# A recurrent cell with two half-states: the order of the DMA queue at a block's edge, and how r and m of the second half are turned and summed

## Chip, cores and metric

One core of one Trainium2 chip runs the whole kernel. The metric is the device time of one execution in microseconds (us); smaller is better.

## The reference

The reference is a gated recurrence over 512 steps, for a batch of 8 and a state of 512, in float32. What is added at the end is the input itself:

```python
def step(h, x_t):
    fused = jax.nn.sigmoid(jnp.concatenate([x_t, h], axis=-1) @ w_W + w_b)
    hidden_state, output_state = jnp.split(fused, 2, axis=-1)
    memory_state = x_t @ wx_W + wx_b + hidden_state * (h @ wh_W + wh_b)
    h_new = output_state * h + (1.0 - output_state) * jnp.tanh(memory_state)
    return (h_new, h_new)
_, hs = jax.lax.scan(step, h0, xT)
return x + jnp.swapaxes(hs, 0, 1)          # x: (8, 512, 512)
```

Below, r is the gate `hidden_state`, z is `output_state`, and m is the memory state before its tanh.

## The kernel before

**Tiling.** The state lies across the 128 partitions in four chunks (KC = 4), two chunks to a half (o = 0 and 1). A step needs products of h with the weights of r, m and z. TensorE (PE) makes them with h as the stationary operand, so that batch rows come out in PSUM in four tiles of 32 rows; VectorE then transposes ("turns") 32x32 blocks so that the state lies across partitions again. r, m and z of the first half, and z of the second, are made with float32 products (line 265). r and m of the second half are made together from h cut into three bfloat16 parts (`products_of_parts`, line 274): their PSUM tile has, for each of 8 batch rows, three rows of partial sums (PARTS = 3), and for m a fourth row with the part of the input x. GpSimd cuts the parts of h (lines 539 and 541) and adds x to h for the output (line 549).

**A step on VectorE.** `turn_r`, `turn_m`, `turn_z(0)`, the scan that forms m of the first half (line 443), then `turn_rm` (line 432, 128 columns of the second half's r and m), `sum_r` (line 439, adds the three parts of r), `mix_h(0)` (line 457, the scan that makes h's first half), `turn_z(1)`, `mix_m_second` (line 449), and `mix_h(1)`. Between them ScalarE computes the sigmoids (lines 359, 363, 366) and tanh (line 372). `turn_rm` writes each turned row so that the four rows of one state element (three parts and x) lie side by side, which puts consecutive output elements four words (16 bytes) apart. `mix_m_second` then runs one scan over 64 columns, four for each of 16 elements: it adds up m's three parts with factors of one, multiplies the sum by sigmoid(r), and adds x's part.

**The order of a step on PE.** It waits for the first half of h, makes its products and those of its parts; waits for the second half of h; makes that half's products (r, m, z0), its parts' products, and z1; last come the products of x for a later group (line 256, `x_products`), which need no h. Then the next step begins.

**Groups and blocks.** Four steps are a group (RING), sixteen a block (STEPS); there are 32 blocks. x's products with the biases added (`xs_biased`, line 462, once a group) are sent by SP's DMA queue to device memory and back (`put_ahead`): one DMA out (`x_rows`, line 188), a wait for its landing, then twelve DMAs back (lines 193 and 197) that bring the rows to `ahead`, from which ScalarE puts them into PSUM (lines 348, 352, 356) before the products of a step are added. SP issues all of this in program order. In a block it issues: the load of x for the block after next into `x_sb` (line 221), the rows of the second group (`put_ahead`, slot 1), then for each group g the loads of `x_grp` (line 206) and the rows of a later group; at the end of the block it waits for GpSimd's sums and stores `y` (line 241). Then the next block's pass begins, with its `x_sb` load and its rows.

Of the kernel before, what the change touches and what calls it, by code (L numbers as in the profile page):

```python
# [6 lines left out]
ALU = mybir.AluOpType  # L7
ACT = mybir.ActivationFunctionType
AX = mybir.AxisListType

P = 128
Q = 32


def build(nc, x, h0, w_h, w_x, b_x, b_h, x_rows, out):
# [49 lines left out]
    with ctx:  # L65
        def sb(name, shape, dt=F32):
            return ctx.enter_context(nc.sbuf_tensor(name, shape, dt))

        def sem(name):
            return ctx.enter_context(nc.semaphore(name))  # L70
# [19 lines left out]
        turned_rm = sb("turned_rm", [P, 2, HB, ROWS])  # L90
        turned_z = sb("turned_z", [P, HALVES, HC, Q])
        pre_r = sb("pre_r", [P, HB])


        m_by = sb("m_by", [P, HB, PAIR])
        m_pre = sb("m_pre", [P, HB, PAIR])
        m_by_parts = sb("m_by_parts", [P, HB, ROWS])
        m_pre_parts = sb("m_pre_parts", [P, HB, ROWS])
# [61 lines left out]
        rm_turned = sem("rm_turned")  # L160
        z_turned = halves("z_turned")
        r_summed = sem("r_summed")
        x_product = sem("x_product")
        x_used = [sem(f"x_used{k}") for k in range(KC - 1)]
        x_biased = sem("x_biased")
# [33 lines left out]
        @block.sync  # L199
        def _(sp):  # L200
            sp.sem_inc(y_stored, 2 * 16)
            x_flat = x.rearrange("p c t b -> p c (t b)")
            out_flat = out.rearrange("p c t b -> p c (t b)")

            def load_x_grp(k, cols):
                sp.dma_start(x_grp[:, k], x_flat[:, k, cols]).then_inc(x_grp_loaded[k], 16)

            sp.dma_start(x_sb[:, :, 0:TOK], x_flat[:, :, 0:TOK]).then_inc(x0_loaded, 16)
            for k in range(KC):
                sp.dma_start(wx[:, k], w_x[:, k]).then_inc(wx_loaded[k], 16)  # L210
# [7 lines left out]
            with sp.Fori(0, BLOCKS) as i:  # L218
                cols = bass.ds(sp.snap((i + 2) % BLOCKS * TOK), TOK)
                sp.wait_ge(x_loaded, sp.snap(i * 16 + 16))  # L220
                sp.dma_start(x_sb[:, :, cols], x_flat[:, :, cols]).then_inc(x_loaded, 16)  # L221


                sp.wait_ge(x_biased, sp.snap(i * PER_BLOCK + 2))
                put_ahead(sp, 1, sp.snap((i * PER_BLOCK + 2) * 16))
                for g in range(PER_BLOCK):

                    turn = sp.snap(i * PER_BLOCK + (g + 1))
                    grp_cols = bass.ds(sp.snap((i * PER_BLOCK + (g + 3)) % GROUPS * GT), GT)
                    for k in range(KC):  # L230
                        if k < KC - 1:
                            sp.wait_ge(x_used[k], turn)
                        else:
                            sp.wait_ge(x_product, sp.snap(i * PER_BLOCK + (g + 3)))
                        load_x_grp(k, grp_cols)
                    if g < PER_BLOCK - 1:
                        sp.wait_ge(x_biased, sp.snap(i * PER_BLOCK + (g + 3)))
                        put_ahead(sp, g % SLOTS, sp.snap((i * PER_BLOCK + (g + 3)) * 16))
                sp.wait_ge(y_added, sp.snap(i * STEPS + 2 * STEPS))
                sp.sem_inc(y_taken, 1)  # L240
                sp.dma_start(out_flat[:, :, bass.ds(sp.snap(i * TOK), TOK)],  # L241
                             y[:, bass.ds(sp.snap(i % 2), 1)].rearrange("p a c t b -> p (a c) (t b)"))\
                    .then_inc(y_stored, 16)
# [102 lines left out]
        def _(act):  # L346
# [9 lines left out]
                act.activation(ps[:, Z_BANK[1], 0:W], ahead[:, slot, t, at:at + W], ACT.Copy).then_inc(z_ahead, 1)  # L356

            def reset_first():
                act.activation(m_by[:, :, 1].rearrange("p (c b) -> p c b", b=B), turned_r[:, :, 0:B], ACT.Sigmoid)\  # L359
                    .then_inc(r_ready[0], 1)  # L360

            def reset_second():
                act.activation(m_by_parts[:, :, PARTS], pre_r[:, :], ACT.Sigmoid).then_inc(r_ready[1], 1)  # L363
# [4 lines left out]

            def new(o, s):
                n_twice = h[:, (s - 1) % RING, o, 1:1 + REGION].rearrange("p (b c w) -> p c b w", c=HC, w=TRI)[:, :, :, 0::2]  # L370
                pre = (m_pre[:, :, 1], m_pre_parts[:, :, PARTS])[o].rearrange("p (c b) -> p c b", b=B)
# [51 lines left out]
        def _(dve):  # L423
# [17 lines left out]
            def mix_m_first():  # L441

                return dve.tensor_tensor_scan(m_pre[:, :, :].rearrange("p i w -> p (i w)"),
                                              m_by[:, :, :].rearrange("p i w -> p (i w)"),
                                              turned_m[:, 0].rearrange("p i w -> p (i w)"), 0.0, ALU.mult, ALU.add)

            def mix_m_second():

                return dve.tensor_tensor_scan(m_pre_parts[:, :, :].rearrange("p i w -> p (i w)"),  # L449
                                              m_by_parts[:, :, :].rearrange("p i w -> p (i w)"),  # L450
                                              turned_rm[:, 1].rearrange("p i w -> p (i w)"), 0.0, ALU.mult, ALU.add)

            def mix_h(o, s, nxt):

# [9 lines left out]
            def step(i, t0, s):  # L464
# [12 lines left out]
                mix_m_first().then_inc(m_pre_ready[0], 1)  # L477
# [3 lines left out]
                sum_r().then_inc(r_summed, 1)  # L481
                mix_h(0, s, nxt)
                dve.wait_ge(z_done[1], nxt)
                turn_z(1).then_inc(z_turned[1], 1)
                dve.wait_ge(r_ready[1], nxt)
                mix_m_second().then_inc(m_pre_ready[1], 1)
                mix_h(1, s, nxt)
                if s % RING == RING - 1:

# [4 lines left out]
                    add_bias(X_BANK)  # L494

            dve.memset(h[:, :, :, :], 0.0).then_inc(start_h, 1)
            dve.memset(m_by[:, :, :], 0.0).then_inc(constants, 1)
            dve.memset(m_by_parts[:, :, :], 0.0).then_inc(constants, 1)
            dve.memset(h_by[:, :, :, :], 0.0).then_inc(constants, 1)
            dve.wait_ge(constants, 3)  # L500
            dve.memset(m_by_parts[:, :, 1:PARTS], 1.0).then_inc(constants, 1)
            dve.memset(h_by[:, :, :, 1], -1.0).then_inc(constants, 1)
            dve.wait_ge(constants, 5)
            dve.wait_ge(h0_loaded, 16)
            dve.wait_ge(start_h, 1)

# [28 lines left out]
        def _(pool):  # L535
# [14 lines left out]
                                   xs_of, hs, ALU.add).then_inc(y_added, 1)  # L550

            pool.sem_inc(y_added, STEPS)
            pool.memset(ahead[:, :, :, :], 0.0).then_inc(ahead_cleared, 1)
            pool.wait_ge(bias_h_loaded, 16)
            pool.wait_ge(ahead_cleared, 1)
# [73 lines left out]
```

## Time and profile before

| | us |
|---|---|
| median of 3 runs | 1673.91 (1670.84 to 1674.57) |
| the profiled execution | 1674.5 |
| its span | 1672.7 |
| PE busy | 1627.8 (97%) |
| VectorE (DVE) busy | 1203.1 (72%) |
| ScalarE (ACT) busy | 890.7 (53%) |
| GpSimd (POOL) busy | 568.7 (34%) |

The busy times are of the profiled execution, and their shares are of its span. PE's busy time includes the modelled ends of its pipelined matmuls, so 97% does not by itself say that PE is the bound; PEld is PE's loading of stationary operands. SPq is SP's DMA queue. The mean granted clock of TensorE over the span was 0.996 of full speed.

### The profile page before, as it was taken

What the parts mean: (1) busy time and instruction counts of PE and PEld (TensorE: products, weight loads), DVE (VectorE), ACT (ScalarE), POOL (GpSimd) and SP (SyncE); (2) the same over time, 40 slices, a digit from 0 to 9 for tenths busy, and PEclk for the clock granted to TensorE, in tenths of its full rate; (3) what the DMA queues carried; (4) which work ended last, traced back from release to release, by engine and by line L of the source; (5) the groups of instructions that cost most, each with busy time, mean ns of one, the idle gap of its engine ahead of it and who ended that gap; (6) DMA issues with size and microseconds to landing.
All of it is one profiled execution on the core that took longest, in us unless ns stands there. A gap on an engine that the chain in (4) does not pass through costs nothing.

```text
span 1672.7 us, 211594 instructions
## 1 busy us (share of the span) xinstructions
PE 1627.8 (97%) x94336; PEld 1343.3 (80%) x94336; DVE 1203.1 (72%) x5272; ACT 890.7 (53%) x4621; POOL 568.7 (34%) x2571
## 2 busy tenths in 40 slices
PE   5999999999999999999999999999999999999998
PEld 3788888888888888888888888888888888888887
DVE  3677777777777777777777777777777777777776
ACT  2455555555555555555555555555555555555554
POOL 1233333333333333333333333333333333333333
PEclk8999999999999999999999999999999999999999
DMA  6111111111111111111111111111111111111111
GB/s 199 32 48 46 51 46 38 51 48 48 46 43 45 46 51 48 46 36 51 49 47 51 46 38 46 52 49 46 35 54 48 46 51 46 38 51 49 48 46 39
DMA packets 194889, 83.27 MB, mean 50 GB/s; under 512 B 123200, under 2 KB 194368, under 8 KB 194880
## 3 DMA queue, kind: packets, MB, share of 16 engines
q1 hardware_dynamic: 193824, 82.47, 18.3%
q10 hardware_dynamic: 1056, 0.67, 0.2%
q8 instruction: 6, 0.10, 0.0%
q14 instruction: 3, 0.02, 0.0%
HBM read 49.30 MB, written 33.75 MB: 50 GB/s over the span
## 4 chain that ended last, share of the span: by engine, by line
PE 72%; DMA 9%; SPq 9%; DVE 4%; issue 3%; ACT 1%; POOL 1%; ACTq 0%; POOLq 0%; DVEq 0%
PE ps L265 43%; PE ps L274 15%; PE ps L256 14%; DMA x_rows<-xs_biased 5%; SPq L197 4%; DMA ahead<-x_rows 3%; SPq L193 2%; SPq L241 1%; SPq L221 1%; DVE h L457 1%; DVE turned_rm L432 1%; DMA wx<-in_w_x 1%; ACT ps L348 1%; DVE m_pre_parts L449 1%; POOL y L549 0%
## 5 line engine op out<-in xcount | busy, mean ns | idle before, releaser
L265 PE MATMUL ps<-wh,h 128*8 128x64 f32 x65536 | 1209.2, 220 | 35.3 <-ACT ps L348 29.2
L265 PEld LDWEIGHTS ps<-wh,h 128*8 128x8 f32 x65536 | 963.2, 93 | 312.6 <-DVE h L457 290.2
L539 POOL TENSOR_TENSOR h<-h 128x16 f32<-128x16 f32 x1026 | 224.7, 219 | 1018.0 <-DVE h L457 1014.1
L274 PE MATMUL ps<-w_parts,h 128*24 128x128 bf16 x24576 | 532.8, 219 | 0.0
L274 PEld LDWEIGHTS ps<-w_parts,h 128*24 128x24 bf16 x24576 | 431.8, 121 | 0.0
L256 PE MATMUL ps<-wx,x_grp 128*32 128x384 f32 x4096 | 425.0, 486 | 0.0
L359 ACT ACTIVATE m_by<-turned_r 128x16 f32<-128x16 f32 x512 | 112.1, 219 | 541.0 <-DVE turned_r L425 541.0
L457 DVE TENSOR_TENSOR_SCAN h<-h_by,h 128x48 f32<-128x48 f32 x1024 | 259.3, 253 | 161.0 <-ACT h L372 161.0
L425 DVE STREAM_TRANSPOSE turned_r<-ps 128x64 f32<-128x64 f32 x512 | 127.8, 250 | 242.6 <-PE ps L265 229.9
L366 ACT ACTIVATE h_by<-turned_z 128x16 f32<-128x16 f32 x1024 | 227.8, 222 | 99.0 <-DVE turned_z L436 63.5
L541 POOL TENSOR_TENSOR h<-h 128x16 f32<-128x16 f32 x1026 | 224.5, 219 | 80.3
L436 DVE STREAM_TRANSPOSE turned_z<-ps 128x64 f32<-128x64 f32 x1024 | 243.1, 237 | 3.0 <-PE ps L265 3.0
L432 DVE STREAM_TRANSPOSE turned_rm<-ps 128x128 f32<-128x128 f32 x512 | 218.2, 426 | 0.2 <-PE ps L274 0.2
L348 ACT ACTIVATE ps<-ahead 128x192 f32<-128x192 f32 x513 | 171.0, 333 | 22.7 <-DMA ahead<-x_rows 22.7
L449 DVE TENSOR_TENSOR_SCAN m_pre_parts<-m_by_parts,turned_rm 128x64 f32<-128x64 f32 x512 | 153.9, 301 | 19.9 <-ACT m_by_parts L363 18.9
L363 ACT ACTIVATE m_by_parts<-pre_r 128x16 f32<-128x16 f32 x512 | 120.8, 236 | 62.2 <-DVE pre_r L439 17.4
L352 ACT ACTIVATE ps<-ahead 128x128 f32<-128x128 f32 x513 | 143.5, 280 | 0.0
L372 ACT ACTIVATE h<-m_pre_parts 128x32 f32<-128x32 f32 x512 | 127.2, 248 | 28.7
L549 POOL TENSOR_TENSOR y<-x_sb,h 128x32 f32 x512 | 138.0, 270 | 0.7
L372 ACT ACTIVATE h<-m_pre 128x32 f32<-128x32 f32 x512 | 124.5, 243 | 0.0
L428 DVE STREAM_TRANSPOSE turned_m<-ps 128x64 f32<-128x64 f32 x512 | 119.7, 234 | 1.7 <-PE ps L265 1.7
L439 DVE TENSOR_REDUCE pre_r<-turned_rm 128x16 f32<-128x48 f32 x512 | 104.1, 203 | 17.6
(30 smaller groups left out, 422.1 us busy)
## 6 DMA issues: line engine op xcount, KB each, us to landing
x_rows<-xs_biased SPq DMA_DIRECT2D x128, 192.0 KB, 1.9
ahead<-x_rows SPq DMA_DIRECT2D x512, 32.0 KB
ahead<-x_rows SPq DMA_DIRECT2D x1024, 8.0 KB
x_sb<-in_x SPq DMA_DIRECT2D x34, 256.0 KB, 3.3
x_grp<-in_x SPq DMA_DIRECT2D x516, 16.0 KB, 1.7
out_h<-y SPq DMA_DIRECT2D x32, 256.0 KB, 2.7
wx<-in_w_x SPq DMA_DIRECT2D x4, 768.0 KB, 9.1
wh<-in_w_h SPq DMA_DIRECT2D x4, 512.0 KB, 7.3
```

Source lines behind the costliest of these rows:

```text
L256: mm = pe.matmul(ps[Q * j:Q * (j + 1), bank, 0:COLS], stands, wx[:, k, j, :], start=(k == 0), stop=(k == KC - 1), tile_position=(0, Q * j))
L265: mm = pe.matmul(ps[Q * j:Q * j + B, bank, 0:W], h_of(s - 1, k), wh[:, k, j, at:at + W], start=False, stop=(k == KC - 1), skip_group_check ...
L274: mm = pe.matmul(ps[Q * j:Q * j + PARTS * B, RM_BANK, 0:2 * W], parts_of(s - 1, k), w_parts[:, k, part, j], start=False, stop=(k == KC - 1 ...
L348: act.activation(ps[:, 0:GATES, 0:W], ahead[:, slot, t, 0:GATES * W].rearrange("p (g n) -> p g n", n=W), ACT.Copy).then_inc(first_ahead, 1)
L366: act.activation(h_by[:, o, :, 2].rearrange("p (b c) -> p c b", c=HC), turned_z[:, o, :, 0:B], ACT.Sigmoid)\
L372: act.activation(n_twice, pre.unsqueeze(3).to_broadcast([P, HC, B, 2]), ACT.Tanh)\
L432: return dve.transpose(turned_rm.rearrange("p g (c b) w -> p (g c) w b", b=B), ps[:, RM_BANK, 0:2 * W].rearrange("p (c q) -> p c q", q=Q))
L436: return dve.transpose(turned_z[:, o], ps[:, Z_BANK[o], 0:W].rearrange("p (c q) -> p c q", q=Q))
L449: return dve.tensor_tensor_scan(m_pre_parts[:, :, :].rearrange("p i w -> p (i w)"), m_by_parts[:, :, :].rearrange("p i w -> p (i w)"), tur ...
L457: dve.tensor_tensor_scan(h[:, s % RING, o, 0:REGION], h_by[:, o].rearrange("p i w -> p (i w)"), h[:, (s - 1) % RING, o, 1:1 + REGION], 0.0 ...
L539: pool.tensor_tensor(mid(1, s, o), mid(0, s, o), mid_top(0, s, o), ALU.subtract).then_inc(left_once[o], 1)
L541: pool.tensor_tensor(mid(2, s, o), mid(1, s, o), mid_top(1, s, o), ALU.subtract)\
```

## The change

Three things are changed.

1. **SP's order at a block's edge.** The pass over a block now begins with the wait for the biased sums and `put_ahead` of slot 1 (the rows); after it come the store of the previous block's `y`, and then the load into `x_sb`. The first block's pass is written out ahead of the loop, and the last block's store stands behind it.
2. **r and m of the second half.** `turn_rm` writes its 128 columns in the order in which they come, adjacent. One reduction (`sum_rm`) adds up the three parts of both r and m: it reads 96 elements, its three terms 8 words (32 bytes) apart, and writes 32. The scan that forms m of the second half has 32 columns instead of 64, like that of the first half.
3. **x's part of m.** Since the scan needs it beside the sum, GpSimd brings it there: in each step, once `turn_rm` is done, it adds zeros to 16 elements of `turned_rm` and writes them into `summed` (`x_moved`). The scan on VectorE waits for that as well as for the sum. On GpSimd this stands ahead of the cutting of h into parts.

```diff
+            def store_y(i, which):
+                sp.wait_ge(y_added, held(sp, i * STEPS + 2 * STEPS))
+                sp.sem_inc(y_taken, 1)
+                sp.dma_start(out_flat[:, :, bass.ds(held(sp, i * TOK), TOK)],
+                             y[:, bass.ds(which, 1)].rearrange("p a c t b -> p (a c) (t b)")).then_inc(y_stored, 16)
+            def pass_of(i, before):
+                sp.wait_ge(x_biased, held(sp, i * PER_BLOCK + 2))
+                put_ahead(sp, 1, held(sp, (i * PER_BLOCK + 2) * 16))
+                if before is not None:
+                    store_y(before, held(sp, before % 2))
+                cols = bass.ds(held(sp, (i + 2) % BLOCKS * TOK), TOK)
+                sp.wait_ge(x_loaded, held(sp, i * 16 + 16))
                 sp.dma_start(x_sb[:, :, cols], x_flat[:, :, cols]).then_inc(x_loaded, 16)
...
+            pass_of(0, None)
+            with sp.Fori(1, BLOCKS) as i:
+                pass_of(i, sp.snap(i - 1))
+            store_y(BLOCKS - 1, (BLOCKS - 1) % 2)
...
             def turn_rm():
-                return dve.transpose(turned_rm.rearrange("p g (c b) w -> p (g c) w b", b=B),
-                                     ps[:, RM_BANK, 0:2 * W].rearrange("p (c q) -> p c q", q=Q))
+                return dve.transpose(turned_rm[:, :, :], ps[:, RM_BANK, 0:2 * W].rearrange("p (c q) -> p c q", q=Q))
...
-            def sum_r():
-                return dve.tensor_reduce(pre_r[:, :], turned_rm[:, 0, :, 0:PARTS], AX.X, ALU.add)
+            def sum_rm():
+                return dve.tensor_reduce(summed[:, :, :, 0].rearrange("p g (c b) -> p (g c) b", b=B),
+                                         turned_rm.rearrange("p c (w b) -> p c b w", b=B)[:, :, :, 0:PARTS],
+                                         AX.X, ALU.add)
...
                 dve.wait_ge(r_ready[1], nxt)
-                mix_m_second().then_inc(m_pre_ready[1], 1)
+                dve.wait_ge(x_moved, nxt)
+                dve.wait_ge(r_summed, nxt)
+                mix_m(1, summed[:, 1]).then_inc(m_pre_ready[1], 1)
                 mix_h(1, s, nxt)
...
                 for s in range(STEPS):
+                    pool.wait_ge(rm_turned, held(pool, t0 + (s + 1)))
+                    pool.tensor_tensor(summed[:, 1, :, 1].rearrange("p (c b) -> p c b", b=B),
+                                       turned_rm[:, HC:2 * HC, PARTS * B:ROWS * B], nothing[:, :, :], ALU.add)\
+                        .then_inc(x_moved, 1)
```

## Rows read from the trace of the kernel before

**Rows 1.** Chain of waits, steady stretch: start us, length us, what.

```profile
920.91 0.34 PE ps L274 x24
...
949.20 0.33 PE ps L274 x24
```

**Rows 2.** Timeline of PE alone: start us, length us, engine line op out<-in.

```profile
903.08 0.51 PE L256 MATMUL ps<-wx,x_grp 128*32 128x384 f32 x4
...
903.40 0.51 PE L256 MATMUL ps<-wx,x_grp 128*32 128x384 f32 x4
903.74 0.25 PE L265 MATMUL ps<-wh,h 128*8 128x64 f32 x4
```

**Rows 3.** Timeline of one step, idle time before in brackets.

```profile
902.55 0.25 DVE L436 STREAM_TRANSPOSE turned_z<-ps 128x64 f32<-128x64 f32 x1
...
902.72 0.18 DVE L443 TENSOR_TENSOR_SCAN m_pre<-m_by,turned_m 128x32 f32<-128x32 f32 x1
...
902.86 0.42 DVE L432 STREAM_TRANSPOSE turned_rm<-ps 128x128 f32<-128x128 f32 x1
...
903.31 0.20 DVE L439 TENSOR_REDUCE pre_r<-turned_rm 128x16 f32<-128x48 f32 x1
903.43 0.25 DVE L457 TENSOR_TENSOR_SCAN h<-h_by,h 128x48 f32<-128x48 f32 x1
...
903.76 0.22 POOL L539 TENSOR_TENSOR h<-h 128x16 f32<-128x16 f32 x1 [1.39 <-DVE h L457]
903.84 0.29 DVE L449 TENSOR_TENSOR_SCAN m_pre_parts<-m_by_parts,turned_rm 128x64 f32<-128x64 f32 x1
...
904.44 0.26 DVE L457 TENSOR_TENSOR_SCAN h<-h_by,h 128x48 f32<-128x48 f32 x1 [0.32 <-ACT h L372]
904.64 0.56 DVE L462 TENSOR_TENSOR xs_biased<-ps,bias_x 128x384 f32<-128x384 f32 x1
...
904.76 0.86 PE L265 MATMUL ps<-wh,h 128*8 128x64 f32 x48
```

**Rows 4.** Chain of waits at the edge of a block.

```profile
905.84 0.66 SPq L241
...
914.82 1.59 DMA ahead<-x_rows
```

**Rows 5.** Who waited for whom: us in total, times, longest us.

```profile
PEld ps L265 <- DVE h L457: 290.2, 509, 1.5
...
PE ps L265 <- ACT ps L348: 29.2, 29, 14.4
ACT ps L348 <- DMA ahead<-x_rows: 22.7, 31, 1.0
```

**Rows 6.** Timeline of SP's queue in an ordinary group.

```profile
918.38 0.33 SPq L188 DMA_DIRECT2D x_rows<-xs_biased  x1
...
923.71 0.65 SPq L197 DMA_DIRECT2D ahead<-x_rows  x2
```

**Rows 7.** Groups by line and shape: xcount | busy us, mean ns | idle before.

```profile
L432 DVE STREAM_TRANSPOSE turned_rm<-ps 128x128 f32<-128x128 f32 x512 | 218.2, 426 | 0.2 <-PE ps L274 0.2
L449 DVE TENSOR_TENSOR_SCAN m_pre_parts<-m_by_parts,turned_rm 128x64 f32<-128x64 f32 x512 | 153.9, 301 | 19.9 <-ACT m_by_parts L363 18.9
...
L425 DVE STREAM_TRANSPOSE turned_r<-ps 128x64 f32<-128x64 f32 x512 | 127.8, 250 | 242.6 <-PE ps L265 229.9
L372 ACT ACTIVATE h<-m_pre_parts 128x32 f32<-128x32 f32 x512 | 127.2, 248 | 28.7
L372 ACT ACTIVATE h<-m_pre 128x32 f32<-128x32 f32 x512 | 124.5, 243 | 0.0
L363 ACT ACTIVATE m_by_parts<-pre_r 128x16 f32<-128x16 f32 x512 | 120.8, 236 | 62.2 <-DVE pre_r L439 17.4
...
L359 ACT ACTIVATE m_by<-turned_r 128x16 f32<-128x16 f32 x512 | 112.1, 219 | 541.0 <-DVE turned_r L425 541.0
L443 DVE TENSOR_TENSOR_SCAN m_pre<-m_by,turned_m 128x32 f32<-128x32 f32 x512 | 104.5, 204 | 0.0
L439 DVE TENSOR_REDUCE pre_r<-turned_rm 128x16 f32<-128x48 f32 x512 | 104.1, 203 | 17.6
...
L462 DVE TENSOR_TENSOR xs_biased<-ps,bias_x 128x384 f32<-128x384 f32 x130 | 72.3, 556 | 6.1 <-PE ps L256 6.1
```

More of the change, by code:

```diff
@@ L89, in build @@
         turned_m = sb("turned_m", [P, ROWS // PAIR, HB, PAIR])
-        turned_rm = sb("turned_rm", [P, 2, HB, ROWS])
+        turned_rm = sb("turned_rm", [P, 2 * HC, Q])
         turned_z = sb("turned_z", [P, HALVES, HC, Q])
[L92 to L98, printed above, removed]
+        summed = sb("summed", [P, 2, HB, PAIR])
+        m_by = sb("m_by", [P, HALVES, HB, PAIR])
+        m_pre = sb("m_pre", [P, HALVES, HB, PAIR])
+        nothing = sb("nothing", [P, HC, B])
         h_by = sb("h_by", [P, HALVES, HB, TRI])
@@ L162, in build @@
         r_summed = sem("r_summed")
+        x_moved = sem("x_moved")
         x_product = sem("x_product")
@@ L217, in _ @@
             sp.dma_start(x_sb[:, :, TOK:2 * TOK], x_flat[:, :, TOK:2 * TOK]).then_inc(x_loaded, 16)
-            with sp.Fori(0, BLOCKS) as i:
-                cols = bass.ds(sp.snap((i + 2) % BLOCKS * TOK), TOK)
-                sp.wait_ge(x_loaded, sp.snap(i * 16 + 16))
+            def store_y(i, which):
[10 more added lines that the diff above has]
+                sp.wait_ge(x_loaded, held(sp, i * 16 + 16))
                 sp.dma_start(x_sb[:, :, cols], x_flat[:, :, cols]).then_inc(x_loaded, 16)
-                sp.wait_ge(x_biased, sp.snap(i * PER_BLOCK + 2))
-                put_ahead(sp, 1, sp.snap((i * PER_BLOCK + 2) * 16))
                 for g in range(PER_BLOCK):
-                    turn = sp.snap(i * PER_BLOCK + (g + 1))
-                    grp_cols = bass.ds(sp.snap((i * PER_BLOCK + (g + 3)) % GROUPS * GT), GT)
+                    turn = held(sp, i * PER_BLOCK + (g + 1))
+                    grp_cols = bass.ds(held(sp, (i * PER_BLOCK + (g + 3)) % GROUPS * GT), GT)
                     for k in range(KC):
@@ L233, in _ @@
                         else:
-                            sp.wait_ge(x_product, sp.snap(i * PER_BLOCK + (g + 3)))
+                            sp.wait_ge(x_product, held(sp, i * PER_BLOCK + (g + 3)))
                         load_x_grp(k, grp_cols)
                     if g < PER_BLOCK - 1:
[L237 to L243, printed above, removed]
+                        sp.wait_ge(x_biased, held(sp, i * PER_BLOCK + (g + 3)))
+                        put_ahead(sp, g % SLOTS, held(sp, (i * PER_BLOCK + (g + 3)) * 16))
+            pass_of(0, None)
+            with sp.Fori(1, BLOCKS) as i:
+                pass_of(i, sp.snap(i - 1))
+            store_y(BLOCKS - 1, (BLOCKS - 1) % 2)
             sp.wait_ge(x_loaded, (BLOCKS + 1) * 16)
@@ L358, in reset_first @@
             def reset_first():
-                act.activation(m_by[:, :, 1].rearrange("p (c b) -> p c b", b=B), turned_r[:, :, 0:B], ACT.Sigmoid)\
+                act.activation(m_by[:, 0, :, 1].rearrange("p (c b) -> p c b", b=B), turned_r[:, :, 0:B], ACT.Sigmoid)\
                     .then_inc(r_ready[0], 1)
             def reset_second():
-                act.activation(m_by_parts[:, :, PARTS], pre_r[:, :], ACT.Sigmoid).then_inc(r_ready[1], 1)
+                act.activation(m_by[:, 1, :, 1], summed[:, 0, :, 0], ACT.Sigmoid).then_inc(r_ready[1], 1)
             def update(o):
@@ L431, in turn_rm, with mix_m @@
             def turn_rm():
-                return dve.transpose(turned_rm.rearrange("p g (c b) w -> p (g c) w b", b=B),
-                                     ps[:, RM_BANK, 0:2 * W].rearrange("p (c q) -> p c q", q=Q))
+                return dve.transpose(turned_rm[:, :, :], ps[:, RM_BANK, 0:2 * W].rearrange("p (c q) -> p c q", q=Q))
             def turn_z(o):
                 return dve.transpose(turned_z[:, o], ps[:, Z_BANK[o], 0:W].rearrange("p (c q) -> p c q", q=Q))
-            def sum_r():
-                return dve.tensor_reduce(pre_r[:, :], turned_rm[:, 0, :, 0:PARTS], AX.X, ALU.add)
[L441 to L451, printed above, removed]
+            def sum_rm():
+                return dve.tensor_reduce(summed[:, :, :, 0].rearrange("p g (c b) -> p (g c) b", b=B),
+                                         turned_rm.rearrange("p c (w b) -> p c b w", b=B)[:, :, :, 0:PARTS],
+                                         AX.X, ALU.add)
+            def mix_m(o, add):
+                return dve.tensor_tensor_scan(m_pre[:, o].rearrange("p i w -> p (i w)"),
+                                              m_by[:, o].rearrange("p i w -> p (i w)"),
+                                              add.rearrange("p i w -> p (i w)"), 0.0, ALU.mult, ALU.add)
             def mix_h(o, s, nxt):
@@ L476, in step @@
                 dve.wait_ge(m_turned, nxt)
-                mix_m_first().then_inc(m_pre_ready[0], 1)
+                mix_m(0, turned_m[:, 0]).then_inc(m_pre_ready[0], 1)
                 dve.wait_ge(rm_done, nxt)
@@ L480, in step @@
                 dve.wait_ge(rm_turned, nxt)
-                sum_r().then_inc(r_summed, 1)
+                sum_rm().then_inc(r_summed, 1)
                 mix_h(0, s, nxt)
@@ L496, in _ @@
             dve.memset(h[:, :, :, :], 0.0).then_inc(start_h, 1)
-            dve.memset(m_by[:, :, :], 0.0).then_inc(constants, 1)
-            dve.memset(m_by_parts[:, :, :], 0.0).then_inc(constants, 1)
+            dve.memset(m_by[:, :, :, :], 0.0).then_inc(constants, 1)
             dve.memset(h_by[:, :, :, :], 0.0).then_inc(constants, 1)
+            dve.wait_ge(constants, 2)
+            dve.memset(h_by[:, :, :, 1], -1.0).then_inc(constants, 1)
             dve.wait_ge(constants, 3)
-            dve.memset(m_by_parts[:, :, 1:PARTS], 1.0).then_inc(constants, 1)
-            dve.memset(h_by[:, :, :, 1], -1.0).then_inc(constants, 1)
-            dve.wait_ge(constants, 5)
             dve.wait_ge(h0_loaded, 16)
@@ L552, in _ @@
             pool.sem_inc(y_added, STEPS)
+            pool.memset(nothing[:, :, :], 0.0).then_inc(ahead_cleared, 1)
             pool.memset(ahead[:, :, :, :], 0.0).then_inc(ahead_cleared, 1)
             pool.wait_ge(bias_h_loaded, 16)
-            pool.wait_ge(ahead_cleared, 1)
+            pool.wait_ge(ahead_cleared, 2)
             for o in range(HALVES):
```

2 lines of the change are left out of this document (1 added, 1 removed).

## Prediction

> **What bounds the kernel now.** I read the chain of waits first, then one step in the timeline, then the list of waits. Away from the edges of a block the chain runs over PE alone: its pieces of one kind return every 3.14 us (from 920.91 to 949.20 are nine steps, 28.29 / 9 = 3.143) [rows 1]. But PE is not alone in front. In PE's timeline [rows 2] the first four of x's matmuls start at 903.08 and the next four at 903.40, so four of them hold PE for 0.32 us; the array is free at 903.72, and the next step's first product starts at 903.74. It starts 0.05 us after the scan that makes the first half of h ends (903.43 + 0.25 = 903.68, [rows 3]). So two cycles have nearly the same length, and the longer sets the pace:
> - PE's own: 3.14 less the 0.02 us of waiting, 3.12 us a step.
> - The first half's loop, 3.14 us: products up to the parts' last (PE), turn r and m (902.86, 0.42 us), sum r (starts 903.31), scan to h (starts 903.43, 0.12 us behind the sum's start), next step. The scan starts while the sum (0.20 us) still drains, so it is VectorE's own queue that sets it.
>
> The second half's loop (sum, sigmoid, scan to m, tanh, scan to h: 903.31 to 904.70) is just in time: PE has issued what needs the first half alone by 904.76 and takes the second half there, 0.06 us after the scan's end (904.44 + 0.26). The table of waits has PE wait for h 509 times in 512 steps, once a step and not twice [rows 5].
>
> At the edge of a block the chain leaves PE [rows 4]: SP issues the store of y (905.84), the load of x_sb, and only then the rows' way out and back, whose last piece flies from 914.82 and lands at 916.41. ScalarE waits for them, 22.7 us in 31 waits or 0.73 each. PE waits for ScalarE's put of them, 29.2 us in 29 waits; without the longest, 14.4 at the start of the program, 14.8 / 28 = 0.53 [rows 5]. I take 0.65 an edge between the two, 31 x 0.65 = 20 us.
>
> **Rows first at the edge.** The rows no longer stand behind the store and the load. xs_biased is summed at 904.64 + 0.56 = 905.20; today 0.64 us pass from there to SP's first issue. In an ordinary group the way takes, from the issue at 918.38 to the last two issues' end at 923.71 + 0.65, 5.98 us [rows 6], and 1.6 to land: 7.6 us. Issued between 905.3 and 905.9, the rows land at 912.9 to 913.5. ScalarE wants them at 916.41 - 0.73 = 915.7: over 2 us to spare. What it is moved past: the store and the x_sb load, 256 KB each, now issue at about 911.5. The store's buffer is free for a block, the x_sb load is for two blocks on, and x_grp's first load, behind them, comes at about 913, where now it comes after the rows' last issue, at 915. Nobody waits for them; if x_grp did come late, PE's x products would, at the group's first step. **Minus 20 us**, between 16 (31 x 0.53) and 23 (31 x 0.73).
>
> **Turning r and m as they come.** The transpose stays at 128 columns but writes runs of adjacent words where it now writes every fourth word. Now: 426 ns for 128 columns, written 16 bytes apart; 250 for 64 columns written adjacent [rows 7]. What do 64 more adjacent columns cost? Between the sum of 48 columns and the bias's 384, VectorE's plain slope is (556 - 203) / 336 = 1.05 ns a column. That gives 250 + 67 = 317, about 108 saved. A bound from the other side: a 64-column transpose frees the engine 0.17 us after its start (902.55 to 902.72, [rows 3]), and the sum does so with 48 columns in 0.12; so a column costs at most (0.17 - 0.07) / 64 = 1.6 ns, the 0.07 being 0.12 less 48 x 1.05. That gives 250 + 102 = 352, 74 saved. A slope of 2.9, as (426 - 250) / 64 would have it, does not fit in the 0.17. I take minus 108; the ends are minus 74 and, if the order of writing doesn't matter at all, 0.
>
> **One sum for both.** The reduction grows from 48 to 96 elements: + 48 x 1.05 = 51 ns. It also reads its three terms 32 bytes apart, where it read them adjacent. No VectorE row reads so. The nearest of another engine: ScalarE's tanh takes 248 ns reading every fourth word against 243 reading every second, 5 ns on 32 reads, while its sigmoid takes 236 writing every fourth word against 219, 17 ns on 16 writes [rows 7]. A spaced read there costs 0.16 ns, a spaced write over 1. By the read, 96 x 0.16 = 15. Upper bounds: 0.84 ns an element, what the spaced write costs the transpose now (108 / 128), or 81; and 3 ns a column, the scans' slope ((301 - 204) / 32), so 96 x 2 = 190. I take + 66, near the low end (below + 51 it can't go, since 48 more elements must be read), because the only pair of rows that tells reads from writes finds reads cheap; range + 51 to + 240.
>
> A page speaks to this. The Trainium skill, "Vector Engine (DVE) Microarchitecture Reference", section 5.2 (Measured stream behaviour on trn2), gives 1.73 ns a column where one source hops at each element and 1.05 in pairs, yet says of a one-source op with one write for two reads that it kept the full read rate. Our sum writes one for three. As an estimate by that page, the first would make the sum + 116, the second + 51; no trace here shows which.
>
> **The short scan** of m shrinks from 64 to 32 columns, 301 to 204 ns: 97 off the second half's loop alone. It gains two waits: for its own sum (long past) and for x_moved. Queued behind them are the scan to h1 and the next step's turns.
>
> **GpSimd's part.** One more operation of 128x16, 0.22 us like its others [rows 3], from 0.08 us after the turn's end (GpSimd's reaction to VectorE, 903.68 to 903.76): it is done 0.30 us after it. The scan needs it 0.55 us after it or later (903.28 to 903.84). Hidden, 0.25 to spare; without that cover each ns counts on the second loop only beyond the 97 + 42 it gains. The next thing in GpSimd's queue, h's parts, waits for a scan that ends later still.
>
> **The sum.** First half's loop: - 108 + 66 = - 42 ns. Second half's: the same - 42 and - 97. PE's own cycle is 20 ns below today's pace, so PE takes over and 20 is all that is won: 512 x 0.020 = 10 us. From the profiled run's 1674.5 (span 1672.7; the median of the runs shown is 1673.9): 1674.5 - 20 - 10 = **1644.5**. Its own range, from 0 to 15 us for the second term (the loop just at PE's pace, or PE without its restart after each wait) and 16 to 23 for the first: 1636 to 1658.
>
> **Rivals.**
> - *The spaced read is dear.* At 0.84 ns an element the sum costs 51 + 81 = 132, the loop grows by 24, 12 us: 1674.5 - 20 + 12 = **1667**. For it: the same engine pays that on the transpose's writes. Against: ScalarE's pair. The first half's loop is the bound again from 0.39 ns on ((108 - 20 - 51) / 96).
> - *The turn does not get shorter (slower).* If its 426 ns are the price of 128 columns and not of spaced writes, the loop grows by 66 to 132 ns, 34 to 68 us: **1689 to 1722**. It decides as soon as the turn saves less than the sum adds, minus 39 ns (20 us / 512). Against it: the 0.17 above.
> - *GpSimd locks the scan out.* mix_h(0) reads two SBUF tensors and would be issued about 0.22 us behind the turn, inside GpSimd's new operation. If it must wait for that, until 0.30 or, with a reaction of 0.03, 0.33: the loop grows by 38 to 68, 19 to 35 us, **1674 to 1689**. Against: in [rows 3] the scan to m starts at 903.84 inside GpSimd's 903.76 + 0.22 and takes 0.29, not above the mean of its kind, 301. The Trainium skill, "SBUF — State Buffer", section "SBUF: two separate sides", has this lock, for a two-input VectorE op against a GpSimd op that reads SBUF. By that rule, this trace does not agree.
> - *The rows still come late.* If something else holds SP or the DMA at the edge, the 20 us stay: **1664**.
>
> **Chances.** Forecast 0.45, dear read 0.25, turn not shorter 0.10, lock 0.06, rows late 0.05, between these 0.09. A measurement of this kernel can tell about 0.2%, 3.3 us. Forecast, rows late, most of the dear read and part of the rest are faster: 0.73; within it 0.10; slower 0.17. The range 1638 to 1686 leaves out the turn that stays long, part of the lock, and a dear read at the scans' price.
>
> **What would show it.** The waits of ScalarE for ahead gone, and step lengths at the edge like the others (else the first step is wrong). turned_rm at 305 to 320 ns (354 still good), the sum at 255 to 280; from 300 on PE waits for h again. PE's first product more than 0.05 us behind h's scan shows PE as the bound. A first scan to h that starts just as GpSimd's new operation ends, and not 0.12 us plus the sum's growth behind the sum, shows the lock.

## The result, and the profile after

The changed kernel takes 1635.61 us (median of 4, 1634.54 to 1637.49) beside 1673.58 (median of 4): a ratio of 0.9781, interval 0.9766 to 0.9796. That is 38 us faster, where 29 were forecast and the range ended at 1638. The profiled execution takes 1637.5 us, its span is 1634.3, against 1674.5 and 1672.7 before.

Groups by line and shape of the changed kernel (xcount | busy us, mean ns of one | idle before), to be held against [rows 7]:

```profile
L440 DVE STREAM_TRANSPOSE turned_rm<-ps 128x128 f32<-128x128 f32 x512 | 162.1, 317 | 0.3 <-PE ps L282 0.3
L446 DVE TENSOR_REDUCE summed<-turned_rm 128x32 f32<-128x96 f32 x512 | 134.5, 263 | 17.4
...
L452 DVE TENSOR_TENSOR_SCAN m_pre<-m_by,summed 128x32 f32<-128x32 f32 x512 | 128.7, 251 | 0.0
...
L574 POOL TENSOR_TENSOR summed<-turned_rm,nothing 128x16 f32<-128x16 f32 x512 | 113.3, 221 | 514.7 <-DVE turned_rm L440 514.7
```

The turn (the transpose `turn_rm`) went from 426 to 317 ns, the number forecast. The sum went from 203 to 263, 60 more where 66 were forecast. The spaced read adds 9 ns to the 51 of the plain elements.

The table of waits has no row left of ScalarE waiting for `ahead`, and PE's wait for ScalarE is the one at the start of the program, against [rows 5]:

```profile
PEld ps L273 <- DVE h L460: 242.5, 509, 0.5
...
PE ps L273 <- ACT ps L356: 14.7, 1, 14.7
```

SP's queue around a block's edge, in the timeline (start us, us, engine line op):

```profile
886.35 0.33 SPq L188 DMA_DIRECT2D x_rows<-xs_biased  x1
888.22 0.30 SPq L193 DMA_DIRECT2D ahead<-x_rows  x1
...
891.67 0.65 SPq L197 DMA_DIRECT2D ahead<-x_rows  x2
892.77 0.65 SPq L221 DMA_DIRECT2D out_h<-y  x1
893.80 0.59 SPq L233 DMA_DIRECT2D x_sb<-in_x  x1
894.67 3.40 SPq L206 DMA_DIRECT2D x_grp<-in_x  x4
```

ScalarE's put that needs these rows starts at 896.72:

```profile
896.72 0.33 ACT L356 ACTIVATE ps<-ahead 128x192 f32<-128x192 f32 x1
```

The rows leave 0.03 us after the biased sums (885.76 + 0.56) and are all issued at 892.32. With 1.6 us to land, that is 2.8 us before the put. The store, the x_sb load and the x_grp loads follow, and nobody waits for them.

One step, against [rows 3]:

```profile
902.57 0.18 DVE L452 TENSOR_TENSOR_SCAN m_pre<-m_by,turned_m 128x32 f32<-128x32 f32 x1
...
902.71 0.32 DVE L440 STREAM_TRANSPOSE turned_rm<-ps 128x128 f32<-128x128 f32 x1
...
903.06 0.26 DVE L446 TENSOR_REDUCE summed<-turned_rm 128x32 f32<-128x96 f32 x1
903.11 0.22 POOL L574 TENSOR_TENSOR summed<-turned_rm,nothing 128x16 f32<-128x16 f32 x1 [0.96 <-DVE turned_rm L440]
903.24 0.25 DVE L460 TENSOR_TENSOR_SCAN h<-h_by,h 128x48 f32<-128x48 f32 x1
...
903.55 0.71 PEld L273 LDWEIGHTS ps<-wh,h 128*8 128x8 f32 x48 [0.48 <-DVE h L460]
903.57 0.87 PE L273 MATMUL ps<-wh,h 128*8 128x64 f32 x48
```

And PE alone, against [rows 2]:

```profile
903.25 0.52 PE L264 MATMUL ps<-wx,x_grp 128*32 128x384 f32 x4
903.57 0.24 PE L273 MATMUL ps<-wh,h 128*8 128x64 f32 x3
```

x's last four matmuls hold the array for 0.32 us, from 903.25 to 903.57, and there the next product starts: no idle array. h was ready at 903.49 and its weights were being loaded at 903.55, 0.02 us before the array was free. Before, scan end to product was 0.054 us (median of all steps), with the loading and the product starting within 0.002 us of each other; now it is 0.077. PE is the bound. Below, a handover is a place where PE takes one half of h; there are two in a step.

The chain of waits, steady stretch, against [rows 1]:

```profile
920.95 0.34 PE ps L282 x24
...
948.86 0.34 PE ps L282 x24
```

Nine steps in 27.91 us are 3.101 each. The prediction stood at 3.122. Over the whole trace I took the 511 distances between the starts of neighbouring turns of r and m. Their sum falls by 39.3 us: 20.0 in the 31 steps at the edges, whose excess over the others is gone; 20.1 in the pace (507 x 0.0396); the first four steps give 0.8 back. The start before the first turn is 1.2 us longer, the end 0.4 shorter, which makes the 38.4 of the spans.

So the question for the experiments: the edge gave what was forecast; why did the pace fall by 40 ns a step and not by 20, and what of the second part brought it?

### The profile page after: what moved, and what is told of

It is laid out like the page before. It is cut to its first block, busy times and chain, and to the rows that moved or that the text cites. A ratio compares the mean times of both kernels' runs of the same rounds, so it can differ in the third digit from the quotient of the medians.

```text
span 1634.3 us, 212603 instructions
## 1 busy us (share of the span) xinstructions
PE 1602.5 (98%) x94336; PEld 1350.6 (83%) x94336; DVE 1146.2 (70%) x5270; ACT 885.2 (54%) x4621; POOL 682.0 (42%) x3084
## 3 DMA queue, kind: packets, MB, share of 16 engines
q1 hardware_dynamic: 193824, 82.47, 18.6%
## 4 chain that ended last, share of the span: by engine, by line
PE 97%; DMA 1%; issue 1%; ACT 0%; ACTq 0%; SPq 0%; DVE 0%; POOL 0%; POOLq 0%; DVEq 0%
PE ps L273 56%; PE ps L282 21%; PE ps L264 20%; DMA wx<-in_w_x 1%; DMA x_rows<-xs_biased 0%; ACTq L197 0%; ACT w_parts L416 0%; ACT w_parts L419 0%; ACTq L193 0%; SPq L210 0%; SPq L208 0%; DVE xs_biased L465 0%; DVE turned_rm L440 0%; DVE summed L446 0%; DVE h L460 0%
## 5 line engine op out<-in xcount | busy, mean ns | idle before, releaser
L273 PEld LDWEIGHTS ps<-wh,h 128*8 128x8 f32 x65536 | 1007.3, 92 | 266.0 <-DVE h L460 242.5
L282 PE MATMUL ps<-w_parts,h 128*24 128x128 bf16 x24576 | 545.0, 219 | 0.0
L282 PEld LDWEIGHTS ps<-w_parts,h 128*24 128x24 bf16 x24576 | 443.3, 121 | 0.0
L574 POOL TENSOR_TENSOR summed<-turned_rm,nothing 128x16 f32<-128x16 f32 x512 | 113.3, 221 | 514.7 <-DVE turned_rm L440 514.7
L380 ACT ACTIVATE h<-m_pre 128x32 f32<-128x32 f32 x1024 | 252.1, 246 | 0.1
L440 DVE STREAM_TRANSPOSE turned_rm<-ps 128x128 f32<-128x128 f32 x512 | 162.1, 317 | 0.3 <-PE ps L282 0.3
L446 DVE TENSOR_REDUCE summed<-turned_rm 128x32 f32<-128x96 f32 x512 | 134.5, 263 | 17.4
L371 ACT ACTIVATE m_by<-summed 128x16 f32<-128x16 f32 x512 | 112.4, 220 | 42.5 <-DVE summed L446 0.4
L452 DVE TENSOR_TENSOR_SCAN m_pre<-m_by,summed 128x32 f32<-128x32 f32 x512 | 128.7, 251 | 0.0
```

Of the source, the lines that this page charges most:

```text
L273: mm = pe.matmul(ps[Q * j:Q * j + B, bank, 0:W], h_of(s - 1, k), wh[:, k, j, at:at + W], start=False, stop=(k == KC - 1), skip_group_check ...
L282: mm = pe.matmul(ps[Q * j:Q * j + PARTS * B, RM_BANK, 0:2 * W], parts_of(s - 1, k), w_parts[:, k, part, j], start=False, stop=(k == KC - 1 ...
L440: return dve.transpose(turned_rm[:, :, :], ps[:, RM_BANK, 0:2 * W].rearrange("p (c q) -> p c q", q=Q))
```

## The experiments

The median of the kernel before was 1679.36 us beside experiments 1, 2, 3 and 11, 1677.51 beside 5 to 8, and 1677.40 beside 4, 9, 10 and 12. Each ratio is held against the one beside it. Where a run is compared with the changed kernel, that is its 1635.6 us of the first comparison; experiments 6 and 7 reach 1634.6 and 1635.4 beside experiments 5 and 8.

A step's length is the mean distance between neighbouring turns in the trace, without the first four and the edges: 3.141 us before and 3.102 in the changed kernel. The mean is needed because the distances alternate wherever VectorE has a share in the pace (before, 3.132 and 3.152): for every second step VectorE's program has one wait more ahead of `turn_r`, for `y_added`, and there `turn_r` starts 0.09 us later behind the second half's first product.

**1. Rows first alone.**

```diff
 (kernel before)
+SP's pass over a block as in the changed kernel
```

> The kernel before with SP's new order at the edge alone. If each part of the change gives what it adds up to by itself: the 31 waits of ScalarE for ahead (0.73 us each) are gone, an edge step is as long as its neighbours (3.15 instead of 3.80), and the time falls by 20 us, to 1653 to 1655 beside 1673.6. Steps inside a block stay at 3.142 us. Rival (the second 20 us of the result also come from SP's order, through DMA traffic that no longer disturbs the steps): steps shorten too, 1636 to 1645.

Measured: 1655.74 us, a ratio of 0.9863 (0.9846 to 0.9879), 23.6 us off. Steps stay at 3.142, and those at the edge are 3.15. The mechanism is as expected, and the rival, in which steps shorten too, is out. The distances between turns add up to 18.6 us less than in the trace of before: 20.0 less at the edges, while the first four steps give back 0.9 and the pace 0.6. The 3.6 us by which the medians differ more than expected go with the median of before, which is 1679.4 here and was 1673.6 in the first comparison; no trace places them.

**2. Everything but rows first.**

```diff
 (changed kernel)
-SP's pass over a block as in the changed kernel
+SP's pass as before
```

> The changed kernel with SP's old order at the edge. Turn, sum, scan and GpSimd's operation alone: steps at 3.102 us as in the changed kernel, 20 us off. The rows' way does not get shorter while four steps before it is needed do, by 4 x 0.04 = 0.16 us, so each of 31 edges loses some 0.16 us more than before (0.8 instead of 0.65): 1673.6 - 20 + 5 = 1658. Rival (the parts just add): 1653.6.

Measured: 1660.76 us, 0.9895 (0.9879 to 0.9912), 18.6 off. Steps 3.102, and at the edges 3.91 instead of 3.79 (means of 31). ScalarE's waits grow to 26.8 / 31 = 0.86 us each, from 0.73:

```profile
ACT ps L348 <- DMA ahead<-x_rows: 26.8, 31, 1.2
```

The edges' excess is 25.0 us instead of 20.0, the 5 expected: the rows' way did not get shorter with the steps. So the two parts bring more together than one by one: the distances between turns fall by 18.6 us with rows first alone, by 15.5 with the rest alone, and by 39.3 with both.

**3. The kernel before with a shorter sum.**

```diff
-                return dve.tensor_reduce(pre_r[:, :], turned_rm[:, 0, :, 0:PARTS], AX.X, ALU.add)
+                return dve.tensor_reduce(pre_r[:, :], turned_rm[:, 0, :, 0:1], AX.X, ALU.add)
```

> The kernel before with SP's new order and with sum_r over one of the three parts of r (two thirds of that sum are left out): 16 elements read instead of 48, 34 ns off the first half's loop and off the second's, nothing else changed. Theory A (PE's own cycle is 3.102 us, because the 3.142 before held 0.02 us of waiting and another 0.02 of restarts after h's weights came just in time or late): steps fall to 3.107, the time to 1673.6 - 20 - 18 = 1636. Theory B (PE's own cycle is 3.122 as the prediction had it, and the other 10 us came from something that only the new turn, scan or GpSimd operation bring): steps stop at 3.122, the time at 1643 to 1644.

Measured: 1646.84 us (0.9812, 0.9795 to 0.9828), 8.9 less than with rows first alone and later than both theories said; steps 3.124. This does not decide: the sum fell from 203 to 182 ns only, 21 and not 34, so that h's loop itself is 3.142 - 0.021 = 3.121 long, just where theory B has its floor. But it shows what waits look like there: the array is hardly idle any more (x's first matmul to the next product 0.647 us, against 0.665 before and 0.645 in the changed kernel), while the stretch from that product to the first product of the parts is still 0.680 us, not 0.670, and the same stretch behind the second half's handover 0.679. It also shows that the first half's loop did set the pace: 21 ns off the sum are 18 off the step.

```profile
L447 DVE TENSOR_REDUCE pre_r<-turned_rm 128x16 f32<-128x16 f32 x512 | 93.2, 182 | 17.6
```

**4. The placing of the turned words alone.**

```diff
 (kernel before, SP's new order)
-                return dve.transpose(turned_rm.rearrange("p g (c b) w -> p (g c) w b", b=B),
+                return dve.transpose(turned_rm.rearrange("p g i w -> p (g i w)").rearrange("p (c q) -> p c q", q=Q),
```

> The kernel before with SP's new order, and of the second part only the placing of the turned words: the transpose writes them adjacent, while sum, scan of 64 and everything else stay as before (so sum and scan take wrong elements; there is no sum for both, no short scan, nothing on GpSimd). The turn should fall from 427 to 317 ns, both of h's loops by 109, so PE is the bound. Theory A (PE's own cycle is 3.102 us; the rest of 3.142 is 0.02 us of an idle array and twice 0.01 of products that follow weights loaded only just then): 3.102, the two stretches from a handover to the next group of products at 0.670 instead of 0.680, and 20 us off beside the rows-first kernel, 1635 to 1636. Theory B (PE's own cycle in the form of before is 3.122): 3.122 and 1645.

Measured: 1636.24 us (0.9758, 0.9742 to 0.9775), steps 3.102. Theory A holds, theory B is out: PE runs the same program as before, and its cycle is 3.102. The halves of h are ready 0.136 and 0.125 us before their products, and both stretches are 0.670 us. In the chain, the pieces of 48 products are 0.67 us each, where in experiment 3 they were 0.67 to 0.69:

```profile
905.89 0.67 PE ps L273 x48
906.90 0.67 PE ps L273 x48
```

```profile
L440 DVE STREAM_TRANSPOSE turned_rm<-ps 128x128 f32<-128x128 f32 x512 | 162.2, 317 | 0.3 <-PE ps L282 0.3
```

The price of the late handovers lies in the first four products of the group, one on each tile: from the first product's start to the fifth's it is 66 ns at the first handover before (64 at the second), and 56 here, as for every later four. So it is in all fourteen traces: 64 to 66 ns where the loading of the weights starts 2 to 4 ns ahead of the first product, and 56 where it starts 23 ns ahead or more.

With sum, scan and GpSimd as before, this one line and the rows first reach 1636.2, and the changed kernel 1635.6. The sum for both, the short scan and GpSimd's operation bring nothing to the time; they are what it takes to make use of words that lie so.

**5. The old placing back in the changed kernel.**

```diff
-                return dve.transpose(turned_rm[:, :, :], ps[:, RM_BANK, 0:2 * W].rearrange("p (c q) -> p c q", q=Q))
+                return dve.transpose(turned_rm.rearrange("p g (c b) w -> p (g c) w b", b=B),
+                                     ps[:, RM_BANK, 0:2 * W].rearrange("p (c q) -> p c q", q=Q))
...  (the tile's shape, and what the sum and GpSimd read of it, follow)
```

> The changed kernel with the old placing of the turned r and m: the transpose writes every fourth word, and the one sum for both reads its three terms adjacent; all else as in the changed kernel. If the order of writing makes the transpose's price: it takes 426 ns again instead of 317, the sum 254 instead of 263 (96 plain elements, 203 + 51), the first half's loop is 100 ns longer than in the changed kernel and, 23 ns of slack under PE taken off and 10 to 20 of restarts added, the steps are 3.19 us: 1635.6 + 45 = 1681. Rival (something else shortened the transpose, such as the tile's place or size): it stays at 317, and the time stays at 1636.

Measured: 1676.47 us, 0.9993 (0.9983 to 1.0002): 41 us slower than the changed kernel, where 45 were expected, with nothing left of its gain. As the rows still go first here, the rest of the second part costs 21 us when the words lie in the old way (1655.7 with rows first alone). Steps 3.183. Turn and sum:

```profile
L440 DVE STREAM_TRANSPOSE turned_rm<-ps 128x128 f32<-128x128 f32 x512 | 217.9, 426 | 0.0
...
L447 DVE TENSOR_REDUCE summed<-turned_rm 128x32 f32<-128x96 f32 x512 | 129.8, 253 | 17.6
```

The order of writing makes the turn's price: the same 128 columns cost 109 ns more with every fourth word. Read adjacent, 96 elements cost 253, so the spaced read of three terms costs 10 ns and not 81.

**6. Without GpSimd's operation.**

```diff
-                    pool.wait_ge(rm_turned, held(pool, t0 + (s + 1)))
-                    pool.tensor_tensor(summed[:, 1, :, 1].rearrange("p (c b) -> p c b", b=B), ...
...
-                dve.wait_ge(x_moved, nxt)
+                dve.wait_ge(x_moved, 1)
+            pool.memset(summed[:, 1, :, 1], 0.0).then_inc(x_moved, 1)      # once, ahead of the loop
```

> The changed kernel without GpSimd's new operation; x's part of m in the second half is left out (zeros stand in its place). If the operation is hidden: same time, 1635.6, steps 3.102, VectorE's scans as long as with it (248 ns beside it, 252 for m). If GpSimd and VectorE hold each other up (a lock on the ports): the scan to the first half of h, issued inside GpSimd's operation, starts or ends sooner, by up to 0.03 us or more; the time would still stay, PE being the bound, but h would be ready 0.03 us or more earlier before PE's first product.

Measured: 1634.64 us (0.9744, 0.9728 to 0.9760), steps 3.102; the scan to h's first half ends 0.076 us before PE's product, with GpSimd's operation 0.077. In the changed kernel that scan starts at 903.24, in the middle of GpSimd's 903.11 + 0.22, and 0.18 us behind the sum's start as without it. The trace shows no lock between these two. The operation is hidden.

**7 and 8. The sums shorter and longer by one term, in the changed kernel.**

```diff
-                                         turned_rm.rearrange("p c (w b) -> p c b w", b=B)[:, :, :, 0:PARTS],
+                                         turned_rm.rearrange("p c (w b) -> p c b w", b=B)[:, :, :, 0:PARTS - 1],   # 7
+                                         turned_rm.rearrange("p c (w b) -> p c b w", b=B)[:, :, :, 0:PARTS + 1],   # 8
```

> The changed kernel with the sums of r and m over two of three parts (a third of each is left out): 64 elements read instead of 96, 34 ns off both loops. PE is the bound: no change, 1635.6, steps 3.102, h ready 34 ns earlier before PE's first product (0.11 instead of 0.077). If h's loop still had a share in the pace, up to 17 us less.

Measured: 1635.38 us (0.9745, 0.9729 to 0.9761), steps 3.102: no change. h is ready 0.114 us before PE's product instead of 0.077. PE sets the pace, and a still shorter loop would bring nothing.

> The changed kernel with the sums over four rows, x's too (m gets x's part twice, r gets the empty row): 128 elements instead of 96, 34 ns more on both loops. h's weights are loaded 0.023 us ahead of the array's being free, so 34 - 23 = 11 ns a step are lost, 6 us; with a restart of PE of 10 ns at the first half's handover, 20 ns and 10 us: 1641 to 1646, steps 3.113 to 3.123. If the loop had over 34 ns of slack: no change.

Measured: 1683.13 us (1.0036, 1.0023 to 1.0048), steps 3.196: 48 us slower than the changed kernel, not 6 to 10. The sum did not grow by 34 ns but by 116:

```profile
L446 DVE TENSOR_REDUCE summed<-turned_rm 128x32 f32<-128x128 f32 x512 | 194.3, 379 | 17.6
```

116 less the slack of 23 (0.077 less the least, 0.054) is 93, and the steps grew by 94: the loop behaves as expected, but the size of the dose was off. The first handover's stretch is 0.680 us again; these 10 ns do not show in the step because the sum starts 0.912 us behind the second half's first product of the parts here and 0.922 in the changed kernel. Why is open. The next two look at the sum's price.

**9 and 10. Four terms, read adjacent, and read 36 bytes apart.**

```diff
 (experiment 5: old placing)                                                     # 9
-                                         ...[:, :, :, 0:PARTS],
+                                         ...[:, :, :, 0:PARTS + 1],
 (experiment 8: sums over four terms)                                            # 10
-        turned_rm = sb("turned_rm", [P, 2 * HC, Q])
+        turned_rm = sb("turned_rm", [P, 2 * HC, ROWS, B + 1])
...  (turn, sum and GpSimd leave out the ninth word)
```

> The kernel with the old, spaced placing and one sum for both, its sum over four rows instead of three (m gets x's part twice): 128 elements read adjacent. If four terms cost what their elements do, the sum takes 253 + 34 = 287 ns and the steps 3.181 + 0.034 = 3.215 us, about 1693. If it is the number of terms that made the spaced sum jump from 263 (three) to 379 ns (four), it takes about 379 here too, and 1740.

> The changed kernel with the sums over four rows and with one unused word behind every eight turned words, so that the four terms lie 36 bytes apart instead of 32. If the spacing's being 32 bytes makes four terms dear (379 ns), the sum falls to about 300 here; if any spaced read of four terms is dear, it stays at about 380. The transpose writes runs of eight words with a gap: 317 ns if a gap between runs is free.

Measured, one execution each: 1693.2 and 1684.9 us, steps 3.217 and 3.200. The sums, of 9 and then of 10:

```profile
L447 DVE TENSOR_REDUCE summed<-turned_rm 128x32 f32<-128x128 f32 x512 | 147.0, 287 | 17.6
```

```profile
L446 DVE TENSOR_REDUCE summed<-turned_rm 128x32 f32<-128x128 f32 x512 | 196.0, 383 | 17.6
```

Adjacent, four terms cost what their elements do, 287. Spaced, they cost 379 at 32 bytes and 383 at 36. So it is neither the number of terms by itself nor the 32 bytes. Two spaced terms took 221 (experiment 7), three 263, four 379. Why the price comes in between three and four is open; I did not try other spacings.

**11. x's products narrowed.**

```diff
-                    last = x_products(s, x_grp[:, s, :])
+                    last = x_products(s, x_grp[:, s, :], width=Q)      # 32 of 384 columns
...  (x_products takes the width)
```

> The changed kernel with x's products made for 32 of their 384 columns (the rest of x's product is left out): PE's own cycle falls by some 0.55 us, so that the steps show the length of the first half's loop. That loop was 3.142 before and lost 48 ns (turn 426 to 317, sum 203 to 263): 3.094 with PE's restarts in it. Theory A expects 3.085 to 3.094 and 1627 to 1632. If the loop had much slack under PE (the scan's end 0.08 us ahead of PE's first product, of which 0.05 is the least seen), 3.07 and below: 1620 or less.

Measured: 1623.30 us (0.9672, 0.9656 to 0.9689), steps 3.079, scan to product 0.054 again. That lies between the two expectations. The first half's loop is 3.079 us long, 23 ns under PE's own cycle, which is the slack seen in the changed kernel (0.077 less 0.054). From the loop of before one comes to 3.141 - 0.048 - 0.008 = 3.085, with 48 ns less from the turn's start to the scan's and 8 ns of late weights at the second handover that are gone; 6 ns are not accounted for. The chain no longer has x's products to follow, and shows the way of this loop:

```profile
900.17 0.27 PE ps L273 x16
900.44 0.02 issue
900.47 0.25 DVE turned_r L433
900.71 0.23 DVE turned_m L436
900.94 0.06 DVE turned_z L443
901.00 0.09 issue
901.09 0.18 DVE m_pre L452
901.27 0.28 DVE turned_rm L440
```

The chain leaves PE after the first 16 of the second half's products, r's, and goes through VectorE's queue: turn r, m and z, the scan of m, and only then the turn of r and m of the second half. But the distances over all steps say that the parts' products still release that turn, as the prediction had it: from the second half's first product of the parts to the sum's start it is 0.912 us in both kinds of step, although `turn_r` starts 0.09 us later in every second one. VectorE's queue is close behind: without a third of these products (the next experiment) the sum starts 0.895 and 0.854 us behind them.

**12. Two of the three parts of the weights.**

```diff
-                    for part in range(PARTS):
+                    for part in range(PARTS - 1):
...  (the last product's flag follows)
```

> The changed kernel with two of the three parts of the weights in the second half's r and m (the third part, the last bits of the float32 weights, is left out): 16 fewer products of 24 columns by 128 a step and half, so 2 x 2 groups of four at 0.056 us, 0.22 us a step off PE's own cycle and off the first half's loop. PE's cycle becomes 3.102 - 0.223 = 2.879. The second half's h, ready 0.08 us before it must be, loses 0.11 of its cover and becomes the bound by 0.03: steps of 2.90 to 2.93 and 1635 - 87 to - 103 = 1532 to 1548. If PE were not the bound, less than half of that.

Measured: 1572.45 us (0.9378, 0.9362 to 0.9393), steps 2.983. This is the fastest kernel of this study, 63 us ahead of the changed one, but it is not the same bargain: r and m of the second half are made with weights that lack their last bits. The 118 ns a step are fewer than the 170 to 200 expected, and now both halves of h end 0.054 us before PE takes them. What sets the pace now is the second half's way through VectorE's queue:

```profile
901.10 0.86 PE L273 MATMUL ps<-wh,h 128*8 128x64 f32 x48
...
901.59 0.25 DVE L433 STREAM_TRANSPOSE turned_r<-ps 128x64 f32<-128x64 f32 x1 [0.54 <-PE ps L273]
...
901.78 0.41 PE L282 MATMUL ps<-w_parts,h 128*24 128x128 bf16 x16
...
902.31 0.29 DVE L440 STREAM_TRANSPOSE turned_rm<-ps 128x128 f32<-128x128 f32 x1
```

The parts' products end at 902.19 and their turn starts at 902.31, 0.12 us later, behind the engine's other work. In the changed kernel the second half's h came 0.137 us before PE's product (0.054 the least), which leaves 0.08, so that this loop was 3.102 - 0.08 = 3.02 long. The third part's products were to take 0.11 off it. They took 0.047, the mean by which the sum starts sooner (0.875 for 0.922), because VectorE's queue is in the way; late weights at this handover give 0.010 back: 3.02 - 0.047 + 0.010 = 2.983. The step of the expectation that failed is this 0.11.

## Why the prediction was off: point by point

- **Rows first.** Right in mechanism and size: 20.0 us in the trace, 0.645 an edge for 0.65, waits gone, 2.8 us to spare.
- **The turn.** Right: 317 ns, 109 off. That the number is met to the nanosecond is in part luck: the same turn took 291 ns in experiment 12, where its products had ended 0.12 us before it, so 317 is not the price of 128 columns alone. The bound from the engine's start-to-start distance, by which a slope of 2.9 ns a column could not be, held: the rival in which the turn does not get shorter is out (experiment 5).
- **The sum.** Right: + 60 for + 66. The rival of the dear spaced read is out for three terms. It was no idle rival, though: with four terms the same read is dear (379), and the kernel slower than before. Of the two statements of the Trainium skill ("Vector Engine (DVE) Microarchitecture Reference", section 5.2) the full read rate fits two and three terms, and 1.73 ns a column fits four: (379 - 153) / 128 = 1.77, with 153 for the fixed part, 203 less 48 x 1.05.
- **GpSimd's part.** Right: hidden, no lock (experiment 6). By the lock of the Trainium skill, "SBUF — State Buffer", section "SBUF: two separate sides", the scan would have waited for GpSimd; the trace does not agree, for these forms.
- **PE takes over, at its own cycle.** Right in mechanism, wrong in size, and this is the miss. "PE's own cycle is 20 ns below today's pace" took off only the time in which the array was idle. Its real cycle is 40 ns below. The other 20 are in the rows of before, in the stretches that I had taken for PE's own work: 0.680 us from the first half's handover to the parts' products instead of 0.670, and 0.678 instead of 0.670 behind the second's. They are there whenever h is ready only 0.054 to 0.057 us before the product, in experiments 3, 5, 8 and 11 at the first handover too, and gone when it comes 0.076 us before or earlier. 3.102 + 0.021 + 0.010 + 0.008 = 3.141. Experiment 4 shows it: beside the rows first, nothing but the turn's writing changed, and the pace went to 3.102. The term was 10 us and measured 20. I had allowed up to 15 for it, "PE without its restart after each wait", so the mechanism was in the prediction, but that puts it at 10 ns a step (5 us / 512) where it is 18, and the forecast itself left it out. The range made the miss worse: the forecast's own began at 1636, the final one at 1638, without a reason, and 1635.6 lies below both.
- **The first half's loop.** Right: 3.079 us in experiment 11, and the parts' products release the turn of r and m in every kernel with three parts. VectorE's queue of the other turns, which the prediction did not have on this way, comes 0.02 us behind them in every second step (0.912 less 0.895).
- **The second half's loop** was said to be in time with nothing to spare. It was (0.056 us before the product), and that was part of the price: its late weights cost 8 ns a step.

## What to carry to other kernels

When a producer's result arrives just as TensorE needs it, subtracting the idle array does not give the engine's own cycle; measure the stretches behind each handover as well, best in a variant in which the producer is early. Where steps alternate, take their mean and not their median: in experiment 12 the median distance is 3.003 us and the mean 2.983, and only the mean fits the time. And a chain of waits that names PE for 97% of the span does so in experiments 5 and 12 too, where VectorE's loops set the pace: the distance from the producer's end to the consumer's start, at its minimum or above it, tells which it is. Write a transposed tile in adjacent words and let the next reader take the stride; but time that reader with its real number of terms.

## What the runs showed of the hardware

- VectorE's transpose of 128 float32 columns from PSUM takes 317 ns when it writes adjacent words (291 in experiment 12) and 426 when it writes every fourth one.
- A reduction to 32 values: 221 ns with two terms 32 bytes apart, 263 with three, 379 with four (383 at 36 bytes); read adjacent, 253 with three and 287 with four.
- Where the loading of the stationary operand starts only 2 to 4 ns before the first product, the first four products take 64 to 66 ns instead of the 56 that they take where it starts 23 ns before or earlier, although the array is hardly idle in between (experiment 3).
